# Two-layer transformer kernel: last conditioning norms on columns, second weight rounded on ScalarE, parameters by span, two banks for picked rows

## The reference

```
def _weight_quant(w):
    scale = 1.0 / jnp.clip(jnp.mean(jnp.abs(w)), 1e-05)
    return jnp.clip(jnp.round(w * scale), -1, 1) / scale
...
cc = jax.nn.silu(c)
h = _bitlinear(cc, wa0, na0)
h = _hgrn_mlp(h, wa1, na1, wa2, na2)
h = _bitlinear(h, wa3, na3, ba3)
h = _rmsnorm(h, wr, 1e-06)
params = _bitlinear(h, wa4, na4, ba4)
s_msa, sc_msa, g_msa, s_mlp, sc_mlp, g_mlp = jnp.split(params, 6, axis=1)
mx = _layernorm(x) * (1 + sc_msa[:, None, :]) + s_msa[:, None, :]
i = _bitlinear(mx, wi, ni)
f = jax.nn.sigmoid(_bitlinear(mx, wf, nf))
```

## Time and profile before

| | us |
|---|---|
| median of 3 runs | 258.57 (258.24 to 261.83) |
| the profiled execution, its time | 259.06 |
| its span from first to last instruction | 257.2 |
| busy: TensorE, VectorE, ScalarE, GpSimd | 155.3, 176.1, 152.1, 78.7 |

### The profile page before, as it was taken

One profiled execution on the slowest core, in us unless ns is written; L12 is line 12 of the kernel. 1 busy time (PEld: TensorE's weight loads), 2 busy tenths in 40 slices (PEclk: granted clock), 3 DMA queues, 4 the chain that ended last, 5 costly groups with the idle time before them and its releaser, 6 DMA issues.

```text
span 257.2 us, 4257 instructions
## 1 busy us (share of the span) xinstructions
PE 155.3 (60%) x1519; PEld 100.6 (39%) x1519; DVE 176.1 (68%) x484; ACT 152.1 (59%) x335; POOL 78.7 (31%) x117
## 2 busy tenths in 40 slices
PE   0220244955741310550738768799999999788985
PEld 0100133544621200310635333366556655354753
DVE  0678777899998696597686568587779787332511
ACT  2655578667864367594513751467668766785431
POOL 7225442111551313388111996011011100103210
PEclk9999999975575555595688997569999999999999
DMA  5997000000000000000000342134000000000011
GB/s 158 401 420 304 0 1 0 3 0 0 1 0 1 0 0 0 0 1 0 3 0 4 97 103 47 28 39 65 6 2 4 4 4 4 2 3 0 3 41 41
DMA packets 4490, 11.49 MB, mean 45 GB/s; under 512 B 1267, under 2 KB 2644, under 8 KB 3828
## 3 DMA queue, kind: packets, MB, share of 16 engines
q1 hardware_dynamic: 3510, 10.04, 11.6%
q0 software_dynamic: 960, 1.19, 1.8%
HBM read 8.24 MB, written 0.52 MB: 34 GB/s over the span
## 4 chain that ended last, share of the span: by engine, by line
DVE 36%; PE 34%; ACT 10%; POOL 8%; issue 5%; DMA 4%; SPq 1%; DVEq 0%; ACTq 0%
DVE negmax L1256 7%; PE ps L1598 5%; PE ps L1389 5%; POOL uh L442 4%; PE ps L1628 3%; PE ps L1634 3%; PE ps L1538 3%; DMA cw<-in_cond_w 2%; PE ps L1479 2%; ACT xhat L658 2%; DVE mx L1148 2%; PE ps L1578 2%; DVE bnst L869 2%; POOL rms L382 2%; PE ps L1372 2%
## 5 line engine op out<-in xcount | busy, mean ns | idle before, releaser
L1256 DVE TENSOR_REDUCE negmax<-ps 128x1 f32<-128x384 f32 (+3 forms) x96 | 51.4, 594 | 15.7 <-PE ps L1540 15.6
L761 ACT ACTIVATE PT<-ps 128x1024 f32<-128x1024 f32 x40 | 39.6, 1033 | 20.7 <-PE ps L1584 20.6
L1538 PE MATMUL ps<-KS,QS 48*128 48x128 bf16 (+3 forms) x128 | 31.7, 324 | 1.0 <-DVE negmax L1256 0.7
L1389 PE MATMUL ps<-k_f,u 128*128 128x128 f32 x40 | 10.0, 426 | 27.9 <-ACT u L648 23.0
L1578 PE MATMUL ps<-QS,KS 51*128 51x512 bf16 (+3 forms) x128 | 24.8, 315 | 1.6 <-DMA QS<-nmT 1.6
L1539 PE MATMUL ps<-k_b 64*128 64x128 bf16 x128 | 24.1, 230 | 0.0
L382 POOL TENSOR_TENSOR rstd<-veps,mhalf 128x4 f32<-128x4 f32 x8 | 8.1, 1014 | 45.8 <-DVE veps L876 45.8
L1540 PE MATMUL ps<-k_b 64*128 64x64 bf16 x128 | 21.5, 197 | 0.0
L1598 PE MATMUL ps<-PT,V 128*9 128x512 f32 (+3 forms) x256 | 20.0, 433 | 1.6 <-DVE attn L1266 1.6
L1389 PEld LDWEIGHTS ps<-k_f,u 128*128 128x128 f32 x40 | 7.6, 220 | 29.9 <-DVE u L1045 27.6
L382 POOL TENSOR_TENSOR rms<-vms,mhalf 128x4 f32<-128x4 f32 x10 | 10.2, 1027 | 28.4 <-DVE vms L1019 28.4
(11 more groups left out here) (209 smaller groups left out, 458.9 us busy)
## 6 DMA issues: line engine op xcount, KB each, us to landing
w<-in_wa SPq DMA_DIRECT2D x2, 1152.0 KB, 10.5
lw<-in_l_w SPq DMA_DIRECT2D x1, 1280.0 KB
brow<-in_bcast_rows SPq DMA_DIRECT2D x1, 1152.0 KB, 15.2
mw<-in_main_w SPq DMA_DIRECT2D x1, 1024.0 KB, 12.9
KS<-part POOLq DMA_DIRECT2D x12, 64.0 KB, 3.2
QS<-part SPq DMA_DIRECT2D x12, 64.0 KB
cw<-in_cond_w SPq DMA_DIRECT2D x1, 576.0 KB, 6.1
xs<-in_x SPq DMA_DIRECT2D x1, 512.0 KB, 7.7
```

The lines of the kernel that those rows point to most:

```text
L761: nc.scalar.activation(PT[n % 2][:, s, :], bank(2 * (use % 2), 2), ACT.Exp).then_inc(S["p_ready"], 1)
L1256: V.tensor_reduce(negmax[n % 2][:, qt, h0:h0 + nh], bank(S_BANKS[k % 3])[:, 0:nh * w].rearrange("p (h w) -> p h w", w=w), AX.X, ALU.max, n ...
L1389: ins = T.transpose(dst[:, tok(t)], src(t), ident)
L1538: T.matmul(dst, QS[b][rows, h, tok(qt)], KS[b][rows, h, 0:w], start=True, stop=False)
```

## The change

It touches five places.

1. wa1 is rounded by two passes on ScalarE, with its own mean, and clipped on VectorE.
2. The input of wa4 is computed on columns: 6 chunks by 2 batches on 128 partitions. wa3's product gives columns at once (6 small matmuls), the sums over the columns are matmuls with ones (`column_sum`), and the maximum is spread by a matmul with the identity. ba3, wr and na4 are loaded as columns.
3. ScalarE's sums of wa4 and its roundings stand in another order; all four rounded chunks come in one row, then the sums of all main weights. wm1 and wm2 are rounded later, behind `to_columns` of the output projection. The cast of k_b moves there too.
4. The parameter product is made in spans of 512 and 256 columns, both batches' 512 first, chunk by chunk as they are ready, and `parameters` follows by span. Batch 0's `ln_apply` stands behind its first span.
5. Group 1's picks go to banks 6 and 1 in turn, and ScalarE's copies of them stand earlier.

```
+W4_ORDER = (0, 3, 1, 4, 2, 5)
...
+PICK_BANKS = (6, 1)
+PICK_AT = (2, 4, 6, 8)
...
-PARAM_BANKS = (0, 6)
+PARAM_BANKS = (0, 5)
...
-            pool.wait_ge(S["half_ready"], 2)
+            pool.wait_ge(S["half_ready"], 3)
...
-            pool.wait_ge(S["half_ready"], 3)
+            pool.wait_ge(S["half_ready"], 4)
...
-            c_root(4, RMS)
-            c_root(5, 4)
+            for n, mean, r in ((4, M_RMS, R_RMS), (5, M_NA, R_NA)):
+                pool.wait_ge(S["c_mean"], n + 1)
+                root(colv_of(r), colv_of(mean)).then_inc(S["c_root"], 1)
...
+            act.wait_ge(S["wa1_inv"], 1)
+            wa1 = slice(*CW["wa1"])
+            nc.scalar.activation(cw[:, wa1], cw[:, wa1], ACT.Copy, bias=MAGIC, scale=winv[:, 1:2]
+                                 ).then_inc(S["wa1_magic"], 1)
+            act.wait_ge(S["wa1_magic"], 1)
+            nc.scalar.activation(cwq[:, wa1], cw[:, wa1], ACT.Copy, bias=-MAGIC).then_inc(S["wa1_rounded"], 1)
...
+            magnitudes4(0)
...
+            magnitudes4(1)
...
+            for c in range(2, 5):
+                magnitudes4(c)
...
+            magnitudes4(5)
...
-            round4(W4_ROUND[0])
-            round4(W4_ROUND[1])
+            for c in W4_ROUND:
+                round4(c)
             act.wait_ge(S["ld_mainw"], 16)
-            for i, name in enumerate(MAIN[:4]):
+            for i, name in enumerate(MAIN):
                 act.wait_ge(S["wsum_ready"], 10 + i)
                 magnitudes(mw[:, slice(*MW[name])], name)
...
+                if i == 3:
+                    act.wait_ge(S["mod_pe"], 1)
+                    nc.scalar.activation(modraw[:, :], bank(4)[:, 16:16 + 4 * B], ACT.Copy).then_inc(S["mod_copied"], 1)
+            def round_main(first, end):
+                for i in range(first, end):
+                    a, z = MW[MAIN[i]]
+                    c = WCOL[MAIN[i]]
+                    act.wait_ge(S["inv_ready"], 2 if i < 4 else 3)
+                    nc.scalar.activation(mw[:, a:z], mw[:, a:z], ACT.Copy, bias=MAGIC, scale=winv[:, c:c + 1]
+                                         ).then_inc(S["main_magic"], 1)
+                for i in range(first, end):
+                    a, z = MW[MAIN[i]]
+                    act.wait_ge(S["main_magic"], i + 1)
+                    nc.scalar.activation(mwq[:, a:z], mw[:, a:z], ACT.Copy, bias=-MAGIC).then_inc(S["main_rounded"], 1)
...
+            round_main(0, 4)
...
             for b in range(B):
                 to_columns(xq3[b][:, 0, :], bank(4 * b + 1), 6 + b)
+            round_main(4, 6)
...
+                if b == 1:
+                    picked_second(0)
...
+                else:
+                    for v in range(1, 4):
+                        picked_second(v)
...
+            c_maximum(0)
+            dve.wait_ge(S["ld_const"], 16)
+            means(0, 1, 1, 1)
+            ternary(weights("wa0"), cw[:, slice(*CW["wa0"])], "wa0")
             c_quantise(0, 1)
-            dve.wait_ge(S["ld_const"], 16)
-            V.tensor_copy(k_b[:, :], k_f[:, :]).then_inc(S["masks_ready"], 1)
-            means(0, 2, 1, 1)
-            ternary(weights("wa0"), cw[:, slice(*CW["wa0"])], "wa0")
...
-            ternary(weights("wa1"), cw[:, slice(*CW["wa1"])], "wa1")
+            means(1, 1, 2, 2)
+            V.reciprocal(winv[:, 1:2], wmean[:, 1:2]).then_inc(S["wa1_inv"], 1)
...
+            means(2, 2, 3, 3)
...
-            means(2, 2, 2, 2)
-            dve.wait_ge(S["ld_x"], 16)
-            ln_stats(list(range(NT)), 1e-6)
+            dve.wait_ge(S["wa1_rounded"], 1)
+            a, z = CW["wa1"]
+            V.tensor_scalar(cwq[:, a:z], cwq[:, a:z], -1.0, 1.0, ALU.max, ALU.min).then_inc(S["wa1_ready"], 1)
...
+            high(weights("wa3"), cw[:, slice(*CW["wa3"])], "wa3", 2)
             c_columns(2)
-            high(weights("wa3"), cw[:, slice(*CW["wa3"])], "wa3", 2)
-            means(10, 1, 3, 3)
-            V.reciprocal(winv[:, 10:11], wmean[:, 10:11]).then_inc(S["inv_ready"], 1)
...
+            means(10, 1, 4, 4)
+            V.reciprocal(winv[:, 10:11], wmean[:, 10:11]).then_inc(S["inv_ready"], 1)
+            def column_mean(i, total, mean, eps):
+                dve.wait_ge(S["c_sum"], i + 1)
+                then(V.tensor_reduce(colv_of(total), bank(6)[:, 32 + 16 * i:32 + 16 * i + OC * B]
+                                     .rearrange("p (c b) -> p b c", b=B), AX.X, ALU.add))
+                V.tensor_scalar(colv_of(mean), colv_of(total), 1.0 / OUT6, eps, ALU.mult, ALU.add
+                                ).then_inc(S["c_mean"], 1)
...
+            dve.wait_ge(S["s3_pe"], 1)
+            then(V.tensor_copy(colv_of(V3), bank(0)[:, 256:256 + B]))
+            dve.wait_ge(S["c_mm"], 4)
+            for b in range(B):
+                ins = V.scalar_tensor_tensor(yc[:, :, b], bank(1)[:, 0:OC * B].rearrange("p (c b) -> p c b", b=B)[:, :, b],
+                                             colv[:, V3, b:b + 1], ccol_of("ba3"), ALU.mult, ALU.add)
+            then(ins)
+            V.tensor_tensor(sqc[:, 0, :, :], yc[:, :, :], yc[:, :, :], ALU.mult).then_inc(S["c_sq"], 1)
+            bn(b0_tiles[2:])
+            column_mean(0, S_RMS, M_RMS, 1e-6)
+            bn(b1_tiles[:2])
+            dve.wait_ge(S["c_root"], 5)
+            then(V.tensor_tensor(gc[:, :, :], yc[:, :, :], over_chunks(colv_of(R_RMS)), ALU.mult))
+            then(V.tensor_tensor(gc[:, :, :], gc[:, :, :], ccol_of("wr").unsqueeze(2).to_broadcast([P, OC, B]), ALU.mult))
+            V.tensor_tensor(sqc[:, 1, :, :], gc[:, :, :], gc[:, :, :], ALU.mult).then_inc(S["c_sq"], 1)
+            then(V.tensor_tensor(uc[:, :, :], gc[:, :, :], ccol_of("na4").unsqueeze(2).to_broadcast([P, OC, B]), ALU.mult))
+            V.tensor_reduce(colv_of(MX_P), uc[:, :, :].rearrange("p c b -> p b c"), AX.X, ALU.max,
+                            apply_absolute_value=True).then_inc(S["c_mx"], 1)
+            clip4(0)
+            column_mean(1, S_NA, M_NA, 1e-8)
+            dve.wait_ge(S["c_mxb"], 1)
+            later(V.tensor_reduce(colv_of(MX), bank(5)[:, 0:B * P].rearrange("p (b n) -> p b n", b=B), AX.X, ALU.max))
+            dve.wait_ge(S["c_root"], 6)
+            settle()
...
+            V.tensor_scalar(cxq[:, :, :], uc[:, :, :], MAGIC, None, ALU.subtract).then_inc(S["c_xq"], 1)
...
             clip4(1)
-            means(4, 4, 4, 4)
+            high4(4)
+            clip4(2)
+            bn(b1_tiles[2:])
+            ln_variance(b0_tiles, 1e-6)
+            ln_variance(b1_tiles, 1e-6)
+            clip4(5)
+            V.scalar_tensor_tensor(dq4[:, :], colv_of(STEP), mean_of("wa4"), colv_of(R_NA), ALU.mult, ALU.mult)
+            means(4, 4, 5, 5)
...
-            means(8, 2, 5, 5)
...
-            ln_apply(list(range(NT)), 1)
...
+                cols = slice((0, 512)[i], (512, OUT6)[i])
+                dve.wait_ge(S["c_mm"], 5 + B * i + b)
+                then(V.scalar_tensor_tensor(par[:, b, cols], bank(PARAM_BANKS[b], 2)[:, cols], dq4[:, b:b + 1],
+                                            brow_of("ba4")[:, cols], ALU.mult, ALU.add))
...
             for b in range(B):
-                if b:
-                    ln_apply(list(range(b * NT, b * NT + NT)), b + 1)
-                parameters(b)
+                parameters(b, 0)
+                if b == 0:
+                    ln_apply(b0_tiles, 1)
                 modulate(b, 0)
+                if b == 0:
+                    parameters(0, 1)
+                    ln_apply(b1_tiles, 2)
+                else:
+                    parameters(1, 1)
...
+                if b == 0:
+                    means(8, 2, 6, 6)
+                    V.reciprocal(winv[:, 8:10], wmean[:, 8:10]).then_inc(S["inv_ready"], 1)
...
+            V.tensor_copy(k_b[:, :], k_f[:, :]).then_inc(S["masks_ready"], 1)
             main_clip(4, 6)
...
-            totals(0, 2, 2)
+            totals(0, 1, 1)
             c_transpose(0)
             c_product(0)
+            pe.wait_ge(S["half_ready"], 1)
+            totals(1, 1, 2)
+            pe.wait_ge(S["half_ready"], 2)
             totals(2, 2, 4)
             c_transpose(1)
+            pe.wait_ge(S["wa1_ready"], 1)
             c_product(1)
             c_transpose(2)
             c_product(2)
             totals(10, OC, 10)
-            c_transpose(3)
-            c_product(3)
-            totals(4, 4, 14)
...
+            c_transpose(3)
+            pe.wait_ge(S["c_scale"], 4)
...
+            pe.wait_ge(S["c_xq"], 4)
+            for c in range(OC):
+                ins = T.matmul(bank(1)[:, c * B:(c + 1) * B], weights("wa3")[:, tok(c)], cxq[:, 0, :],
+                               start=True, stop=True)
+            ins.then_inc(S["c_mm"], 1)
+            def column_sum(i):
+                pe.wait_ge(S["c_sq"], i + 1)
+                T.matmul(bank(6)[:, 32 + 16 * i:32 + 16 * i + OC * B], ones[:, :],
+                         sqc[:, i, :, :].rearrange("p c b -> p (c b)"), start=True, stop=True).then_inc(S["c_sum"], 1)
```

(33 more changed lines are left out.)

171 lines of the change are left out of this document (70 added, 101 removed).

## The result

The changed kernel takes 261.5 us (260.26 to 262.07), the kernel before 258.82 beside it; the ratio is 1.0098 with a 95% interval of 1.007 to 1.0126. By the ratio that is 2.5 us more, where 5.6 were forecast. The profiled execution took 261.65, with a span of 259.8 against 257.2: +2.6.

| place | before | forecast | after | gained or lost since the row above |
|---|---|---|---|---|
| first layer's row | 14.38 | 12.4 | 11.16 | |
| third product's row | 28.30 | 25.4 | 23.84 | |
| scale of the last weight out | 28.37 | 31.0 | 29.09 | |
| batch 0's parameters | 48.55 | 49.1 | 46.42 | −2.13 (forecast +0.6) |
| batch 1's norms | 61.20 | 64.1 | 61.41 | +2.34 (+2.3) |

The account below looks back on a forecast made before the run. No one engine was taken to bound the whole; each stretch was read for its last wait. +0.6 + 2.3 + 4.3 − 1.6 = +5.6 took the span from 257.2 to 262.8, median 264.2 us (range 262.3 to 266; 8 in 10: 260.0 to 267.2).

Parts of the forecast that it names:

- the sum's first term: End of the conditioning: batch 0's parameters formed at 49.1 instead of 48.55 us, +0.6.
- Up to the second product: Conditioning's start: first layer's row out at 12.7 instead of 14.7, second product over at 18.6, nothing gained.
- the small loads are worth nothing: Two small loads changing size (18 KB less, 9 KB more): no effect, ScalarE's first sum being set by a later-landing weight.
- From there to the scale: Second product to last weight's scale: third row 2.9 us earlier, then lost; scale out at 31.0, 2.6 later than before.
- The column stage: Last weight's input on columns: second column sum waits behind the main weights' total; parameter product's inputs ready at 43.4.
- From the inputs to the parameters: VectorE's steps from the parameter product's inputs: 5.7 us, parameters formed at 49.1.
- Behind the parameters: From parameters to batch 1's norms: VectorE's work grows by 2.3 us; norms start at 64.1 instead of 61.20.
- The late rounding: Two big main weights rounded behind batch 1's columns: VectorE's clip waits, residual starts at 94.7 instead of 90.39, +4.3.
- The picks: First group's maxima: two banks and earlier copies spare TensorE's waits, −1.6 us, at most 1.8.
- Rival 1: Column stage not held: inputs at 39.6 instead of 43.4, 3.8 less, median 260.4 us; chance 0.14.
- Rival 2: Late rounding half hidden: the clip costs 1.0, median 260.9 us; chance 0.08.
- rival 3: More contention (clip pays 0.65) and slow TensorE delaying batches by 1, picks gain 0.5 only: 267.0 us; chance 0.14.

Follow-up runs that it names:

- the split columns: Changed kernel with the small columns' load cut to 7 KB in its old place, the other 9 KB loaded behind all else: 261.81 us, ratio 1.0104.
- the padded kernel before: Kernel before with its load of small columns padded from 7 to 16 KB by values that nothing reads: 259.90 us in one run.

## Why the prediction was right and wrong

The direction was right. The size was not: +5.6 was forecast, +2.6 came in the span. Most of the miss is the sum's first term, the parameters at +0.6, which came at −2.13. Of these 2.7, the first layer's row gave 1.2, the steps from it to the scale 0.7, and those from the inputs to the parameters 0.8. The other terms were held to 0.6, and what the sum left out altogether (+1.19) worked against the miss.

*Up to the second product: the step that failed.* The first layer's row was put out at 12.7 and came out at 11.50 (11.16 + 0.34). It started 3.2 before the row of before, not 2.0. The 2.0 for the passes is right (13.19 against 11.16 when they were put back). What failed is the wait ahead of them. I took the row of before and subtracted the passes, and so kept what that row waits for. The kernel before:

```profile
6.43 0.20 ACT L504 ACTIVATE scT<-ccol 128x2 f32<-128x2 f32 x1 [1.47 <-DMA ccol<-in_cols]
...
7.01 0.31 ACT L492 ACTIVATE junk<-cw 128x128 f32<-128x128 f32 x1
...
8.64 1.16 ACT L492 ACTIVATE junk<-cw 128x1152 f32<-128x1152 f32 x1 [1.22 <-DMA cw<-in_cond_w]
...
14.38 0.34 DVE L942 TENSOR_SCALAR cy<-ps,cs 2x128 f32<-2x128 f32 x1
```

There one total serves wa0 and wa1, so the row starts 5.73 or 5.74 behind wa1's sum (8.64) in all five profiles of the kernel before and its variants. The change gives wa0 a total of its own. The row now starts 6.07 or 6.08 behind ScalarE's silu of the small columns in all eleven profiles whose wa1 is rounded on ScalarE, while wa1's sum starts anywhere from 7.60 to 8.26. The silu matters because it stands in ScalarE's queue ahead of wa0's sum, which follows it by 0.58 or 0.59 in all seventeen profiles. With the landing of the profile of before, 6.43, this would give 12.5, nearly the forecast 12.4; the silu came at 5.08, 1.35 earlier. So the sentence of the prediction that the small loads are worth nothing, since ScalarE's first sum is set by a weight that lands later, read the rows wrongly: the sum that waits for a weight is the second, wa1's; the first, wa0's, waits for the columns. The loads' sizes are indeed worth nothing, but the landing had become what the row waits for, and I took it from one profile of another kernel. That it would be 1.35 earlier no row ahead of the change showed, and why it is stays open.

*From there to the scale.* The order held: ScalarE's last sum, the total (0.59), the modulation products (1.85), the transposition. They only started from a sum that ended at 25.6 instead of 27.2. So the scale was out at 29.09, 0.7 later than before and not 2.6. The product was over at 17.19 (16.07 + 1.12) instead of 18.6, and the path gained the other 0.5 between the product and the scale.

*The column stage* was held as forecast, behind ScalarE's roundings (6.9 from 29.13, 6.85 forecast) and four sums (1.65 from there to the total at 37.68, 1.7 forecast), and for the reason forecast: taking the total out of the way gave 3.4. The quantised columns came at 41.50 instead of 43.4, all of it by the earlier scale: from scale to columns it took 12.4, as forecast. The place is a loss of 3.4 against a better order. It hides in the ratio, since the columns still come 1.95 before those of the kernel before (41.33 against 43.28).

*From the inputs to the parameters* I had 5.7, it took 4.9: the variances take 0.97 together instead of 1.2, and the clips and steps overlap at their ends (0.27 for a clip and 0.93 for a step from start to start, for 0.35 and 0.99). With the 1.9 from the steps ahead this makes the 2.7 by which the parameters beat the forecast.

*Behind the parameters* +2.34 came for +2.3. *The late rounding* cost 3.7 in the profile and 3.8 alone, for 4.3: the two adding passes took 1.75 us together and the two subtracting ones 1.56, where I had 1.85 and 1.66, and they started 0.2 earlier against batch 1's norms. *The picks* gave 1.98 for 1.6, past the bound of 1.8. Against the first maxima GpSimd's additions started 1.33 earlier (at 160.88 behind 154.17, and at 157.11 behind 149.07 before) where I had 1.2, and the split followed them at once instead of 0.59 later. That TensorE's clock in this stretch was 0.95 and not 0.85 belongs to it: with one bank at full clock the stretch took 10.47, so by that profile some 0.65 of the 1.98 went with the clock.

*Left out altogether:* +1.19 at the first query and key products. It doesn't come with any part of the change that was tried. In seventeen profiles they took 1.98 or 1.99 in seven and 3.67 to 3.78 in ten, and which it is doesn't follow from the edits as far as one profile each can show: the split columns had 1.98 from 141.35 where the changed kernel had 3.68 from 141.81, and the padded kernel before 3.78 from 137.36 where before had 1.99 from 137.94. So of the +2.6 in the span, about 1.2 may be one execution's chance; how much of it is in the +2.5 of the medians, no profile shows. The two profiles that there are of one program (the kernel before with the late rounding) agree, with 3.78 in both.

*The rivals.* Rival 1 (not held) didn't happen, though the time came nearer to its 260.4 than to 264.2; that is luck for it, since the column sum was held by the total. Rival 2 (half hidden) didn't: the wait was 3.47. Of rival 3 the contention did show: the new clip of 1152 columns, beside GpSimd's thresholds from 12.93 on, took 0.70 in the changed kernel (0.69 or 0.70 in all eleven profiles that have it), where the estimate from 0.55 for 1536 columns was 0.45. The trace agrees with the rule of the Trainium skill (GPSIMD Engine Reference, Key points) that the prediction named, at some 0.25 and not 0.65; in which mode the clip ran no trace shows.

```profile
12.93 4.08 POOL L405 TENSOR_SCALAR cwq<-cw,whalf 128x640 bf16<-128x640 f32 x2
...
15.32 0.70 DVE L1002 TENSOR_SCALAR cwq<-cwq 128x1152 bf16<-128x1152 bf16 x1
```

## What to carry to other kernels

When work is taken off an engine at the head of a chain, ask at once what the chain hangs on next; if it is a load, its landing in another kernel's profile is a number with a spread of its own (here 1 us), and a sum built on it carries it to the end. Work that is moved to "where there is time" has to be laid against the queue that waits for it: 3.2 us of ScalarE's passes cost 3.8 in one place and nothing in a stretch of 4.3 us some 16 us earlier. And a small instruction for a later stage (a total of 0.59 us) that stands between two steps of the path in an in-order queue costs what its own input is late, here 3.4.

## What was not expected of the hardware

- The granted clock of TensorE in the same stage differs between profiles of kernels that are alike up to a load's size (four products in 1.98 or in 3.78 us), and costs 1.2 to 1.3 us there. The span's granted clock also differs between runs of one kernel: 0.846 to 0.856 in the six of the changed kernel.
- With one bank the picks' stretch is longer where the granted clock is lower (10.47 us at 1.00, 12.19 at 0.72), though not by its mean alone (11.55 at 0.70). With two banks it took 9.13 or 9.14 in eleven profiles, none of which had a clock under 0.95.
- A load of 7 or 16 KB lands 2.8 to 3.3 us after its issue in the variants of the changed kernel and 3.8 to 4.4 in those of the kernel before, whatever its size and that of the first load. The load of 392.5 KB issued just ahead of it is early and late with it.
- The kernel before with the late rounding had a granted clock of 0.816 over the span in both of its profiles, where the others had 0.84 to 0.87; why is open.
